# Reordering three queues of a software-pipelined decoder layer: roots among scatters, exponentials and copies on ScalarE, products on TensorE

## The reference

```python
x = layernorm(x + dilated_attention(x))            # 16 heads, segments of 64, every second token of a segment
x = layernorm(x + xattn(x, ctx, Wq, Wkv, Wout))    # 16 heads, causal, keys and values from ctx (64 features)
x = layernorm(x + moe(x, gate_w, w_gate, w_up, w_down))   # 32 experts, top 8, capacity 1024 rows each
```

## Time and profile before

| | |
|---|---|
| median of 3 runs | 600.43 us (600.2 to 601.47) |
| the profiled execution's own time | 601.89 us |
| its span, first to last instruction | 600.1 us |
| PE / DVE / ACT / POOL busy, share of the span | 85 / 66 / 56 / 65 % |
| PE / DVE / ACT / POOL busy in the 16.75 us from 128.84 us | 14.72 / 13.30 / 10.63 / 10.58 us |
| granted TensorE clock there, share of 2.4 GHz | 1.00 |

### The profile page before, as it was taken

The page is one execution under the profiler, slowest core; times in us unless marked ns, Lnnn a source line. Parts: engine busy times, 40 slices in busy tenths (PEclk is TensorE's granted clock), DMA queues, the critical chain, the costliest instruction groups (busy, mean ns, idle before and its releaser), DMA issues.

```text
span 600.1 us, 16476 instructions
## 1 busy us (share of the span) xinstructions
PE 511.5 (85%) x4567; PEld 407.5 (68%) x4568; DVE 393.8 (66%) x1571; ACT 334.6 (56%) x1208; POOL 387.4 (65%) x596
## 2 busy tenths in 40 slices
PE   2789898888888888888517999999999999995894
PEld 2556555565556555554206999999999999994683
DVE  1368777877778777886343666666666666664875
ACT  2265666667665655666303666666666767671112
POOL 6542766566666766655671888888888878883433
PEclk9999999999999999999756999999999999997999
DMA  9299999997122222222234666666666666666995
GB/s 196 78 330 269 284 346 376 342 337 251 69 76 87 87 76 76 77 73 84 93 126 141 202 202 187 194 195 205 185 201 196 186 198 185 199 195 262 427 419 184
DMA packets 79835, 118.48 MB, mean 197 GB/s; under 512 B 12339, under 2 KB 69565, under 8 KB 77760
## 3 DMA queue, kind: packets, MB, share of 16 engines
q1 hardware_dynamic: 63456, 78.63, 43.6%
q0 software_dynamic: 13824, 37.78, 17.0%
q10 hardware_dynamic: 2528, 1.74, 1.0%
HBM read 56.07 MB, written 66.22 MB: 204 GB/s over the span
## 4 chain that ended last, share of the span: by engine, by line
PE 45%; POOL 16%; issue 12%; DVE 12%; DMA 7%; ACT 6%; POOLq 1%; SPq 0%; DVEq 0%; ACTq 0%
PE bank L804 17%; POOL queues L539 11%; PE bank L820 11%; PE bank L796 6%; DMA wall<-results 5%; ACT pr L900 4%; PE bank L814 3%; DVE kP L1073 3%; PE bank L618 1%; POOL rz L502 1%; PE bank L608 1%; POOL rz L496 1%; DVE nmax L1050 1%; PE bank L669 1%; DMA cs<-in_ctx 1%
## 5 line engine op out<-in xcount | busy, mean ns | idle before, releaser
L563 POOL DMA_INDIRECT results<-ys,wcol x152 | 150.5, 990 | 26.0 <-POOL pscrap L552 23.8
L539 POOL DMA_INDIRECT queues<-x,xidx x128 | 128.2, 1002 | 37.0 <-issue 37.0
L804 PE MATMUL bank<-wall,xtT 128*128 x624 | 129.3, 330 | 0.0
L900 ACT ACTIVATE pr<-bank,nmax 128x128 f32<-128x128 f32 x256 | 90.9, 371 | 28.1 <-DVE nmax L1050 28.1
L804 PEld LDWEIGHTS bank<-wall,xtT 128*128 128x128 f32 x624 | 99.4, 193 | 0.1
L820 PE MATMUL bank<-wall,hT 96*128 x304 | 90.7, 379 | 0.0
L991 ACT ACTIVATE ys<-bank,wcol 128x256 f32<-128x256 f32 x152 | 72.1, 474 | 27.8 <-PE bank L820 27.8
L1261 DVE SCALAR_TENSOR_TENSOR tg<-th,bank 128x96 f32<-128x96 f32 x156 | 39.6, 254 | 58.2 <-ACT th L985 58.2
L796 PEld LDWEIGHTS bank<-ident,xt 128*128 128x128 f32 x314 | 61.7, 197 | 20.5 <-DMA xt<-queues 12.7
L796 PE MATMUL bank<-ident,xt 128*128 128x128 f32 x314 | 63.0, 281 | 12.0 <-DMA xt<-queues 12.0
L608 PE MATMUL bank<-kP,qS 128*128 128x512 f32 x128 | 66.2, 599 | 0.0
(11 more groups left out here) (189 smaller groups left out, 890.8 us busy)
## 6 DMA issues: line engine op xcount, KB each, us to landing
xt<-queues SPq DMA_DIRECT2D x162, 160.0 KB
results<-zeros SPq DMA_DIRECT2D x16, 1024.0 KB
wall<-results SPq DMA_DIRECT2D x16, 1024.0 KB, 19.8
queues<-zeros SPq DMA_DIRECT2D x2, 1760.0 KB
wall<-in_L_ffn_w_gate SPq DMA_DIRECT2D x4, 768.0 KB
wall<-in_L_ffn_w_up SPq DMA_DIRECT2D x4, 768.0 KB
wall<-in_L_ffn_w_down SPq DMA_DIRECT2D x4, 768.0 KB
results<-ys,wcol POOLq DMA_INDIRECT x152, 2.9
```

What stands on the lines that cost most here:

```text
L539: pool.indirect_dma_start(xg, bass.IndirectOffsetOnAxis(ap=xidx[:, par, k:k + 1], axis=0), x2[:, par, :], None, bounds_check=last_row, oob ...
L563: pool.indirect_dma_start(yr, bass.IndirectOffsetOnAxis(ap=wcol[:, u, 1:2], axis=0), ys[:, u, :], None, bounds_check=last_y, oob_is_err=Fa ...
L804: ins = pe.matmul(bank[2 + u % 2][:, 0:2 * INTER].rearrange("p (g i) -> p g i", g=2), xtT[:, u % 2, kk, :], wall[:, bass.ds(e, GU)].rearrange(
L900: ins = act.activation(pr[:, g % 2, q, :], pS[g % 2][:, q * P:(q + 1) * P], ACT.Exp, bias=nmax[:, 4 * g + q:4 * g + q + 1], accum_out=den[ ...
```

## The change

On GpSimd `ct` is split from `gm` (`context`) and goes behind the wait for `xidx`; `keep` goes in front of that wait, behind a wait of its own for x2; `root_a` goes behind the fifth scatter, two behind `root_r`, where it was behind the sixth. On ScalarE `exps(b, 2)` goes ahead of `probs_T(b, 1)`, and the end of the step becomes `rT`, `exps_A(a+1)`, `exps(a, 0)`. On TensorE the dilated product (L669) goes ahead of `values(b, 0)`; its wait for `eAT` goes between the two products of `scores(b, 2)`. No instruction is added or removed, and no shape changes. The line numbers of the changed program are some lines higher.

```diff
-        actB = Steps(sem("actB"), "e1 T0 T1 e2 T2 e3 T3 rT")
+        actB = Steps(sem("actB"), "e1 T0 e2 T1 T2 e3 T3 rT")
...
             pool.tensor_tensor(gm[:, par, :], ..., own[:, :], ALU.mult).then_inc(poolA.sem, 1)
+
+            def context(a, par):
                 pool.tensor_copy(ct[:, par, 0:LAT], ...).then_inc(poolA.sem, 1)
...
                     mask_x(a + 2, par)
+                    if r is None:
+                        context(a + 2, par)
...
                     last = isinstance(r, int) and r == NB - 1
+                    if not last:
+                        pool.wait_ge(dveN.sem, dveN.at(r + 2, "x2"))
+                        keep(r, par)
                     if isinstance(r, int) and r == 0:
                         pool.wait_ge(queues_init, 16 * (INIT + 1))
                     pool.wait_ge(dveR.sem, dveR.at(r, "idx"))
-                    if not last:
-                        keep(r, par)
+                    if a is not None and not (isinstance(a, int) and a >= NB - 2):
+                        context(a + 2, par)
                     for k in range(TOPK):
                         if k == 3 and not (isinstance(r, int) and r == NB - 1):
                             root_r(r + 3)
-                        if k == 6 and not (isinstance(r, int) and r >= NB - 3):
+                        if k == 5 and not (isinstance(r, int) and r >= NB - 3):
                             root_a(r + 3)
...
-            def scores(b, g, par):
+            def scores(b, g, par, also=None):
...
+                if also is not None:
+                    pe.wait_ge(*also)
                 pe.matmul(pS[g % 2][:, :], qS[:, g % 2, m, :], kP[:, par, m, :, :], ...)
...
-                    scores(b, 2, pb)
-                if a is not None:
-                    pe.wait_ge(dveA.sem, dveA.at(a, "turn"))
-                if b is not None:
-                    if there(b - 1):
-                        pe.wait_ge(dveY.sem, dveY.at(b - 1, "add"))
-                    values(b, 0, pb)
+                    scores(b, 2, pb, None if a is None else (dveA.sem, dveA.at(a, "turn")))
                 if a is not None:
+                    if b is None:
+                        pe.wait_ge(dveA.sem, dveA.at(a, "turn"))
                     for j in range(PAIRS):
...
                 if b is not None:
+                    if there(b - 1):
+                        pe.wait_ge(dveY.sem, dveY.at(b - 1, "add"))
+                    values(b, 0, pb)
                     turn_probs(b, 1, None)
...
                     exps(b, 1)
                     probs_T(b, 0)
+                    exps(b, 2)
                     probs_T(b, 1)
-                    exps(b, 2)
...
-                if a is not None:
-                    exps(a, 0)
                 if b is not None:
                     act.wait_ge(peB.sem, peB.at(b, "rT"))
                     act.copy(flat2(rT[:, :, :]), pO[:, D:2 * D]).then_inc(actB.sem, 1)
                 if a is not None and not (isinstance(a, int) and a == NB - 1):
                     exps_A(a + 1)
+                if a is not None:
+                    exps(a, 0)
```

More of the change, by code:

```diff
@@ L439, in _ @@
             mask_x(0, 0)
+            context(0, 0)
             put(pool.memset, kP[:, :, :, :, :].rearrange("p a m q k -> p (a m q k)"), 0.0)
@@ L508, in step @@
                     mask_x(1, 1)
+                    context(1, 1)
                     root_a(0)
```

## The result

The changed kernel takes **581.86 us** (four runs, 580.39 to 583.85) against 600.35 of the kernel before on the same chip: ratio 0.969, 95% interval 0.9653 to 0.9728, 18.5 us less. The forecast was 585.3, its range 583 to 592: the direction holds and the two loops are there, but the gain is 3.4 us larger than forecast and the time 1.1 us outside the range.

The account below looks back on a forecast made before the run. Two closed loops of nearly equal length, GpSimd's and TensorE's with ScalarE, bound the front stage. Gains of 11.85 (eleven steps), 1.94 (two more), 0.96 (short step) and 0.40 (last scatters) sum to 15.15 us: 585.3 us, range 583 to 592.

Parts of the forecast that it names:

- the two loops: Front stage, `xidx` to `xidx`: GpSimd's closed loop, 16.76 us, and one through TensorE and ScalarE, 16.64; the change shortens both.
- the length of the new step: Front stage: 15.68 us, the TensorE and ScalarE loop after the change; eleven steps gain 11.85 us.
- the first two steps: Start of the front: gain put at 0, between a loss and a gain of one shift of 1.2 us.
- the second loop: TensorE and ScalarE, `xidx` to `xidx`: 16.64 falls to 15.68, group 0's transposition 0.52 earlier, group 2's 0.44 wait gone.
- GpSimd's 14.53: GpSimd's loop after the change: `root_a` 7.71 after `xidx`, x1 0.62 later, then 6.20 to the next `xidx`.
- breaking one loop alone gains 0.12 a step: Front stage: whoever breaks only one of the two loops gains 0.12 us a step.
- the exchange of products: TensorE: dilated product and group 0's values change places at no cost, if copy `prT` and `eAT` are in time; otherwise 0.44.
- `keep`'s 0.40: GpSimd, last two tiles' scatters behind the short step: `keep`'s 0.40 us was to be gained whole.
- GpSimd's copy holds VectorE up: Rival, chance 0.12: `ew` on VectorE waits for all of moved `keep`, 0.40 a step, 590.9 us.
- Only half of the second loop: Rival, chance 0.11: group 0's transposition stays, only group 2's 0.44 wait goes; step 16.20, 592.5 us.
- Nothing moves: Rival, chance 0.05: variances come no earlier, GpSimd's loop stays, only the last 0.40 is left; 600.0 us.
- Slower: Rival, chance 0.04: group 0's exponentials wait for `sA`; if it came 1.4 later, step 17.08, 604.8 us.

Follow-up runs that it names:

- e3: Changed kernel with x1's root back behind the sixth scatter instead of the fifth: 586.94 us, ratio 0.9783, step 15.82.
- e1: Kernel before with GpSimd's part of the change alone (`context`, moved `keep`, x1's root one scatter earlier): 597.84 us, ratio 0.9953, step 16.59.
- e4: Changed kernel with group 0's exponentials first again on ScalarE, ahead of `rT` and the dilated exponential: 593.35 us, ratio 0.99, step 16.38.
- e5: Changed kernel with group 2's exponentials behind the second copy `prT` again on ScalarE: 590.02 us, ratio 0.9829, step 15.99.
- e2: Kernel before with ScalarE's two reorderings alone: 586.59 us, ratio 0.9758, step 15.82.
- e6: Changed kernel with TensorE's order of before, group 0's values ahead of the dilated product: 586.75 us, ratio 0.9774, step 15.84.
- e9: Control: changed kernel with its loop one pair of steps shorter and two more steps written out: 581.29 us, ratio 0.9697, step 15.49.
- e10: The control e9 with `gm` issued one step earlier, between the seventh and eighth scatters: 582.47 us, ratio 0.9683, step 15.48.
- e11: The control e9 with both `gm` between the scatters and the router's exponential ahead of x1's transposed copy: 578.65 us, ratio 0.9628, step 15.33.
- e8: Changed kernel with the router's exponential `er` ahead of x1's transposed copy on ScalarE: 579.7 us, ratio 0.9666, mean step 15.39.
- e7: Changed kernel with the dilated exponential behind group 0's on ScalarE (`rT`, `exps(a, 0)`, `exps_A`): 585.74 us, ratio 0.9756, step 15.90.

## Why the prediction was right, and where it was wrong

**The step that failed** is the length of the new step. The sum has 15.68, and the sign of being right was 15.6 to 15.9; measured are 15.49 in the eleven steps and 15.53 in the two in front of them. Over thirteen steps that is 2.4 us, of the 3.4 by which the gain was larger than forecast; the range, down to 583, left 1.1 us for it beside the 1.2 of the first steps. What was mis-sized in the 15.68 is told below. Next comes the term for the first two steps, put at 0: the trace of the change is 1.04 ahead there.

**Right: the two loops.** Predicted was 15.68 a step as 2.85 + 7.28 + 3.15 + 2.40; measured in the step shown 2.85 + 7.12 + 3.08 + 2.47 = 15.52. GpSimd's loop was put at 14.53; in e3, where it binds with one scatter more, the step is 15.82, and less that scatter's 1.27 it is 14.55. e1 and e3 show each loop as the bound when the other is broken, e4 and e5 the two steps of the second loop's gain.

**Partly luck: GpSimd's 14.53.** `keep` off the path and `ct` onto it was to gain 0.15 in front of `root_r`. It gained nothing: the first scatter starts 1.04 after `xidx` as before, since the idle time in front of it grew from 0.30 to 0.46 (GpSimd, before and after):

```profile
128.84 1.03 POOL L539 DMA_INDIRECT queues<-x,xidx  x1 [0.30 <-issue]
```

```profile
137.26 1.02 POOL L548 DMA_INDIRECT queues<-x,xidx  x1 [0.46 <-issue]
```

So `root_r` starts 4.64 after `xidx` and not 4.48; but from there to `root_a` are 3.12 and not 3.23, and the two misses nearly cancel (7.76 for 7.71).

**Wrong: breaking one loop alone gains 0.12 a step.** For GpSimd's part that held (e1, 0.18), for ScalarE's it did not (e2, 0.95). The two loops are not independent: GpSimd's 16.76 held 0.81 of waiting for the variance of x2, which comes by way of TensorE, so whoever shortens the second loop shortens the first as well (in e2 `root_r` starts 4.63 after `xidx` on average, 5.51 before). The prediction has the 0.81 in its rows, but not in this sentence; the sum of the whole change does not use it.

**Wrong, the size of a step, by 0.19 (2.2 us in eleven steps).**
- From group 0's transposition to x1's I took 7.72 less the 0.44 of idle. Group 2's transposition came 0.52 closer to group 1's (e5 gives the same 0.52 back): an idle time in a row is not the shift of a start. And the way from there to x1's fell from 1.92 to 1.82: before, x1 ended at 138.83 and its transposition started at 138.89, so those 0.10 were a wait for GpSimd's root, the other loop's time in a duration that I took for this one's. Against these stand 0.02 between groups 0 and 1.
- From x1's transposition to `ew` were 3.27 in the rows, because VectorE ran late behind x1 (e2 and e3, where x1 waits for its root, have 3.24 and 3.27 too). I left that out and took 3.15; it became 3.08, as in e1. Of these last 0.07, 0.05 lie between the start of the transposition, which takes 0.38 and not 0.44, and that of its copy on ScalarE (0.42, 0.47 before); the rest lies in `er` and the way to `ew`. The 0.44, too, is a row in which TensorE had just waited for x1.

From `ew` to `xidx` it became 0.07 more: `keep` runs beside `ew`, which takes 0.23 and not 0.17. Together 0.08 + 0.10 - 0.02 + 0.07 - 0.07 = 0.16 in the step shown; the mean of the eleven is 0.03 lower still.

**Wrong, the exchange of products costed at nothing.** The sum came out, because its cover held. But the sentence that the first copy `prT` is there in time was false: without the exchange the copy is late, and the step is 0.35 longer (e6). What I called free pays for the lateness that ScalarE's new order brings.

**Wrong, the first two steps taken at 0.** TensorE's timeline in the second step, of before and of the change:

```profile
29.72 0.66 PE L618 MATMUL bank<-ident,pr 128*128 128x128 f32 x4
...
36.76 0.66 PE L618 MATMUL bank<-ident,pr 128*128 128x128 f32 x4 [0.66 <-ACT pr L900]
```

```profile
31.27 0.66 PE L630 MATMUL bank<-ident,pr 128*128 128x128 f32 x4 [1.26 <-ACT pr L911]
...
36.42 0.66 PE L630 MATMUL bank<-ident,pr 128*128 128x128 f32 x4
```

Group 0 is transposed 1.55 later, as feared, but the wait in front of group 2 is gone, and group 2 comes 0.34 sooner; the next step gains 0.7 more. My bound of a gain, 1.2, took this in; the value did not. How much of it is the change's, one trace of each doesn't tell: the first `xidx` starts at 58.69 in the change, and in e9 and e3, which have the same order up to there, at 58.49 and 57.66 (59.73 before).

**Not in the prediction: a hole that is no part of the change.** Of the 3.39 in the next two steps, 1.06 is a stop in the dilated product of before that waits for nothing the trace shows:

```profile
65.18 0.77 PE L669 MATMUL bank<-gm,eAT 64*64 64x32 f32 x20
67.02 0.54 PE L669 MATMUL bank<-gm,eAT 64*64 64x32 f32 x12 [1.06 <-issue]
```

The change has none there. Five of the thirteen traces of this case have one (before 1.06, e1 0.46, e2 1.20, e5 0.68, e10 1.58), and in these five a packet of the instruction queue is moved between 63.0 and 65.0 us; the other eight have it by 62.0 at the latest. That TensorE stops for a late fetch of instructions fits; it was not tested by itself, and one trace of each kernel doesn't tell whether the stop goes with the build or with the execution. So e1, e2, e5 and e10 carry a loss that their edits don't explain, and steps are compared behind it. In e10 it is more than the stop: TensorE's granted clock is at its lower level, 1.2 GHz, for most of the 3.5 us that follow (0.55 of 2.4 GHz from 67.3 to 70.8), and the product of queries and keys takes 1.91 where it takes 1.02 otherwise:

```profile
67.61 1.91 PE L622 MATMUL bank<-kP,qS 128*128 128x512 f32 x2
```

e10's first step is 18.84, 3.3 longer than in e9.

**Wrong, `keep`'s 0.40 at the last tiles.** The first scatter of tile 14 started 0.78 after `xidx` with `keep` between them and starts 0.68 after it without: 0.10 was gained, and 0.07 of it was lost again in the idle time behind that scatter, 2.14 before and 2.21 after.

**The expert stage, taken as unchanged.** Its gain of 1.60 in the pair lies where TensorE's granted clock rises from its lower level, 1.2 GHz (busy times PE, PEld, DVE, ACT, POOL, then PEclk, DMA share, GB/s; before, then after):

```profile
300.00:320.00 20.00, 3.56 (x17) 1.99 (x18) 6.54 (x44) 0.89 (x4) 11.87 (x14) 0.50 0.40 138
320.00:340.00 20.00, 20.00 (x114) 19.23 (x113) 10.19 (x44) 11.79 (x37) 10.52 (x18) 0.87 0.58 170
```

```profile
280.00:300.00 20.00, 3.60 (x17) 2.10 (x17) 6.54 (x44) 0.87 (x5) 12.13 (x14) 0.50 0.40 135
300.00:320.00 20.00, 19.99 (x122) 19.13 (x121) 11.41 (x51) 12.71 (x40) 11.53 (x20) 0.94 0.62 183
```

In both TensorE is nearly idle for the 20 us in front, at 0.50 of 2.4 GHz; behind them it is granted 0.87 in before and 0.94 in the change. By an estimate from these two rows the rise comes 5.2 and 2.4 us into them, 21.5 and 18.4 behind the last `xidx`: 3.1 us more at half the clock, which makes 1.6 us. The code there is the same, and e9 to e11 take 294.7 to 295.8 us for this part: it varies by more than 1 us anyway, and I don't count it to the change.

Together 2.19 + 0.24 in the steps, 2.49 at the start, 1.60 in the expert stage, less 0.37 for `keep`: 6.15 us more than forecast in the pair. Of these 2.8 are the choice of executions (1.5 above one median, 1.2 below the other); the 3.4 between the medians are left. Without the stop (1.06) and the expert stage (1.60) the traces leave 3.5, close to that. Each excess was small, and all but `keep`'s had one sign: I bounded waits that might come up, and hardly the waits of before that would go besides the two named.

**The rivals.** *GpSimd's copy holds VectorE up*: the mechanism is there, but nearly hidden. In the change the scan takes 0.88 beside `gm` (0.28 in e10) and `ew` 0.23 beside `keep`; 0.07 shows in this step, and 0.03 on average, not the 0.40 that was priced. Where the two meet more fully `ew` costs 0.14 (e4) to 0.18 (e8) a step. The Trainium skill (SBUF — State Buffer, section "SBUF: two separate sides") has a VectorE instruction with two inputs from SBUF shut out while GpSimd reads SBUF, if GpSimd started first. The scan and `ew`, with such inputs, agree by their ends: the scan ends 0.09 behind `gm`, `ew` 0.06 behind `keep`. As to who is first, the rows agree where the lead is clear: in e4 and e7 the scan starts 0.10 to 0.17 ahead of `gm` and takes 0.28 to 0.34. In the change it starts 0.01 to 0.03 ahead and is held all the same, so the rows do not show a lead as small as that rightly, or the rule does not hold for it. *Only half of the second loop*: that is e4 (16.38, priced at 16.20). *Nothing moves*: the step fell by 1.28. *Slower*: `sA` ended 0.94 after `xidx`, as in the rows.

**Open.** The four runs of the change lie near 580.5 and near 583.5, and only one near 580.5 left a trace. A stop as in e10 would fit: it cost 3.3 us, and the mean granted clock of e10's traced run is 0.948, as in the change's two longer runs (0.950 and 0.951 in the two others). No trace of such a run of the change shows it.

## What to carry to other kernels

When two closed loops have almost one length, a repair of one alone can measure as little (GpSimd's, 0.5%) and hide what it is worth, and the other as much (ScalarE's, 2.4%), because a loop may hold a wait for the other one. Add both loops up, look in each for such waits, and undo parts in the kernel that has both. A duration between two events of the bounding step may hold a share of the other loop's wait: look at what released each of its ends before carrying it over. And a part that is worth nothing alone can be the cover of another (the exchange of products): test it in the kernel that has all the others.

## What was not expected of the hardware

A scan over 128x32 numbers on VectorE went from 0.28 to 0.88 us beside a product of 0.75 on GpSimd, so it matters in a tuned order which small instruction meets which. The scatters do it too: `pickb` went from 0.18 to 0.69 beside one. And TensorE stopped for 0.46 to 1.58 us within one row of products in five of thirteen traces, and in one of them ran at its lower clock behind the stop, 3.3 us in all: more than some of the parts compared here.
